# Token rows scattered as high and low fp16 halves, expert blocks loaded with a transposing transfer

## What is computed

```python
x = x + _layernorm(_L0_attn_ref(_layernorm(x, axis=-1), ...), axis=-1)
x = x + _layernorm(_L0_ffn_ref(_layernorm(x, axis=-1), ...), axis=-1)

# in _L0_ffn_ref: 8 experts, HIDDEN = 512, TOP_K = 2
shared = jnp.einsum('th,hd->td', jax.nn.silu(x_flat @ shared_w1.T), shared_w2.T)
top_k_gates, top_k_idx = jax.lax.top_k(x_flat @ gate_w.T, TOP_K)
top_k_gates = jax.nn.softmax(top_k_gates, axis=1)
h = jnp.einsum('td,ehd->teh', x_flat, experts_w1)
expert_out = jnp.einsum('teh,edh->ted', jax.nn.silu(h), experts_w2)
selected = jnp.einsum('ted,te->td', expert_out, gates)
return (shared + selected).reshape(B, S, D)
```

## Time and profile before

| | us |
|---|---|
| median of three runs | 606.42 |
| the profiled execution | 603.52 |
| its span, first to last instruction | 601.8 |
| TensorE busy | 465.4 |
| VectorE busy | 295.8 |
| GpSimd busy | 272.3 |
| ScalarE busy | 261.4 |

### The profile page before, as it was taken

The page is one execution under the profiler, slowest core; times in us unless marked ns, Lnnn a source line. Parts: engine busy times, 40 slices in busy tenths (PEclk is TensorE's granted clock), DMA queues, the critical chain, the costliest instruction groups (busy, mean ns, idle before and its releaser), DMA issues.

```text
span 601.8 us, 10616 instructions
## 1 busy us (share of the span) xinstructions
PE 465.4 (77%) x3392; PEld 360.3 (60%) x3392; DVE 295.8 (49%) x1258; ACT 261.4 (43%) x540; POOL 272.3 (45%) x408
## 2 busy tenths in 40 slices
PE   4799999999979998698625765597999899997000
PEld 3477766667655666476314544476999899887000
DVE  5887785786571477995444302300323222222273
ACT  3554544444544466554543312233444344443043
POOL 7200000110001366678878875500555655556593
PEclk9899999999999999988668877778999999999555
DMA  8920000000000000001010221345222222221621
GB/s 269 329 92 19 19 19 1 2 1 1 2 0 1 1 2 0 2 2 36 19 33 28 64 71 54 122 117 173 65 72 75 83 77 74 72 64 40 249 115 70
DMA packets 23221, 38.09 MB, mean 63 GB/s; under 512 B 4384, under 2 KB 14880, under 8 KB 22912
## 3 DMA queue, kind: packets, MB, share of 16 engines
q1 hardware_dynamic: 13248, 23.78, 12.2%
q0 software_dynamic: 4544, 9.45, 4.8%
q10 hardware_dynamic: 5376, 4.20, 2.1%
HBM read 21.74 MB, written 15.66 MB: 62 GB/s over the span
## 4 chain that ended last, share of the span: by engine, by line
PE 53%; POOL 17%; DVE 9%; another core or an unknown queue 7%; issue 6%; ACT 5%; DMA 2%; POOLq 0%; ACTq 0%; DVEq 0%; SPq 0%
POOL xs L505 5%; PE pPQ L895 4%; PE pPK L613 4%; PE pQKV L895 4%; PE pKV L688 3%; PE pPK L611 3%; PE pF L613 3%; PE pF L611 3%; PE pPK L612 3%; PE pF L612 2%; PE pQKV L811 2%; PE pPK L804 2%; POOL rs L449 2%; PE pQKV L857 2%
## 5 line engine op out<-in xcount | busy, mean ns | idle before, releaser
L578 POOL DMA_INDIRECT ys<-MID,PQT x78 | 75.7, 971 | 25.6 <-issue 25.6
L445 POOL TENSOR_TENSOR ve<-mv,eps 128x4 f32<-128x4 f32 x40 | 8.0, 201 | 164.8 <-DVE mv L1117 164.7
L505 POOL DMA_INDIRECT xs<-PL,SLOT x64 | 62.8, 981 | 19.8 <-issue 19.8
L611 PE MATMUL pPK<-XFH,E1H 128*128 128x512 f16 x32 | 15.5, 484 | 45.1 <-ACT HT L1041 25.5
L449 POOL TENSOR_TENSOR rs<-ve,halves 128x4 f32<-128x4 f32 x40 | 40.7, 1018 | 3.1
L438 POOL TENSOR_TENSOR held<-halves 128x1 f32<-128x1 f32 x47 | 9.1, 194 | 67.9 <-DVE MID L1424 58.6
L895 PE MATMUL pQKV<-E,HT 128*128 x320 | 39.1, 275 | 0.5 <-DVE MID L1424 0.5
L1424 DVE TENSOR_SCALAR MID<-pPQ,PQT 128x128 f32<-128x128 f32 x38 | 11.6, 346 | 55.7 <-remote 39.3
L895 PEld LDWEIGHTS pQKV<-E,HT 128*128 128x128 f32 x320 | 37.3, 192 | 1.0 <-issue 0.7
L895 PE MATMUL pPQ<-E,HT 128*128 x304 | 37.1, 275 | 0.4 <-DVE MID L1424 0.4
L895 PEld LDWEIGHTS pPQ<-E,HT 128*128 128x128 f32 x304 | 35.4, 192 | 0.9 <-issue 0.7
(11 more groups left out here) (258 smaller groups left out, 1309.2 us busy)
## 6 DMA issues: line engine op xcount, KB each, us to landing
PQT<-xs SPq DMA_DIRECT2D x39, 132.0 KB
PQT<-in_ew1T SPq DMA_DIRECT2D x1, 2304.0 KB, 10.7
E<-in_ew2T SPq DMA_DIRECT2D x1, 2304.0 KB, 10.6
X<-in_x SPq DMA_DIRECT2D x8, 256.0 KB, 6.0
HT<-in_ew1T SPq DMA_DIRECT2D x8, 256.0 KB, 5.9
sh<-PK ACTq DMA_DIRECT2D x8, 256.0 KB
PQT<-sh SPq DMA_DIRECT2D x8, 256.0 KB, 3.9
PQT<-ys SPq DMA_DIRECT2D x4, 512.0 KB
```

Source lines behind the costliest of these rows:

```text
L505: eng.indirect_dma_start(xs, bass.IndirectOffsetOnAxis(SLOT[:, g, t, a:a + 1], 0), PL[:, g, t, a, :], None).then_inc(s_scat[g], 16)
L578: eng.indirect_dma_start(ys, bass.IndirectOffsetOnAxis(XS[q][:, t, ID_AT:ID_AT + 1].bitcast(U32), 0), Y[q][:, t, :], None).then_inc(s_ysc[ ...
L611: nc.tensor.matmul(o, a[0], b_[0], start=True, stop=False)
```

## The change

- The token rows in `PL` now hold the fp16 high halves of 128 numbers, then the 128 low halves, in the same 512 bytes. At stage 14 VectorE writes the fp32 token into slot 1, and ScalarE writes its high half into slot 0. At stage 15 VectorE writes the low half there; at stage 16, once TensorE has transposed slot 1, VectorE copies high and low to slot 1. Scatters are the same in count and size.
- A block's load becomes two transfers: gates and row numbers only (16 bytes a row, 256 pieces), and a transposing transfer of the 256x256 halves into a ring `XB` of four blocks, which lies in `PK`. The transfer waits until the up-projection of four blocks ago is done.
- `turn_block`, `hi_block` and `lo_block` are gone; the up-projection waits for the transfers.
- SyncE's wait for the shared results' stores moves from behind the eighth load to ahead of the first.
- A partition now holds rows p and 128 + p of a block rather than 2p and 2p + 1.

```diff
+RING = 4
+    xs16 = xs.bitcast(F16)
-        XBH, XBL = (PK[:, i].rearrange("p c f -> p (c f)").bitcast(F16)[:, 0:2 * BW].rearrange("p (q s) -> p q s", q=2) for i in range(2))
+        XB = PK[:].rearrange("p i c f -> p (i c f)").bitcast(F16)[:, 0:RING * 2 * BW].rearrange(
+            "p (q i s) -> p q i s", q=RING, i=2)
+        PLH = PL[:].rearrange("p g t a w -> p (g t a w)").bitcast(F16).rearrange(
+            "p (g t a w) -> p g t a w", g=GB, t=T, a=TOPK)
...
@@ sync @@
             sp.wait_ge(s_tab, 13)
+            for h in range(2):
+                sp.wait_ge(s_shst[h], 16 * (NG // 2))
             for k in range(NBLK):
...
-                sp.dma_start(XS[q], xs[bass.ds(row, BW)].rearrange("(p a) w -> p a w", a=2)).then_inc(s_bx[q], 16)
+                sp.dma_start(XS[q][:, :, D:RW],
+                             xs[bass.ds(row, BW)].rearrange("(t p) w -> p t w", t=2)[:, :, D:RW]).then_inc(s_bx[q], 16)
+                wait(sp, s_u, 2 * (k - RING) + 2)
+                sp.dma_start_transpose(XB[:, k % RING], xs16[bass.ds(row, BW), 0:2 * D]).then_inc(s_bx[q], 16)
                 if k == UNROLL - 1:
-                    for h in range(2):
-                        sp.wait_ge(s_shst[h], 16 * (NG // 2))
...
@@ tensor @@
-                    turn(pKV, lambda t: PL[:, g, t, 0, 0:D]).then_inc(s_fT, 1)
+                    turn(pKV, lambda t: PL[:, g, t, 1, 0:D]).then_inc(s_fT, 1)
...
-            def turn_block(k):
-                q = k % UNROLL
-                wait(pe, s_bl, k - 1)
-                pe.wait_ge(s_bx[q], k // UNROLL * 16 + 16)
-                for t in range(2):
-                    m = nc.tensor.transpose(turned[k % 2][:, t * P:(t + 1) * P], XS[q][:, t, 0:D], ident[:])
-                m.then_inc(s_bT, 1)
...
-                    m = three(o, w, [XBH[:, k % 2, :], XBL[:, k % 2, :]])
+                    m = three(o, w, [XB[:, k % RING, i, :] for i in range(2)])
...
-                pe.wait_ge(s_bl, k + 1)
-                if k + 1 < NBLK:
-                    turn_block(k + 1)
+                pe.wait_ge(s_bx[k % UNROLL], k // UNROLL * 32 + 32)
                 up_block(k, ew)
@@ scalar @@
-                    A(PL[:, g, :, 1, 0:D], PL[:, g, :, 0, 0:D], ACT.Copy).then_inc(s_cpy, 1)
+                    A(PLH[:, g, :, 0, 0:D], PL[:, g, :, 1, 0:D], ACT.Copy).then_inc(s_rh, 1)
...
-            def hi_block(k):
-                wait(act, s_u, 2 * k - 2)
-                act.wait_ge(s_bT, k + 1)
-                A(XBH[:, k % 2, :], (pT, pKV)[k % 2][:, 0:BW], ACT.Copy).then_inc(s_bh, 1)
@@ vector @@
-                    norm(4, n, lambda t: PL[:, g, t, 0, 0:D], row(X, n))
+                    norm(4, n, lambda t: PL[:, g, t, 1, 0:D], row(X, n))
...
+                if k == 15:
+                    dve.wait_ge(s_rh, n + 1)
+                    v.tensor_tensor(PLH[:, g, :, 0, D:2 * D], PL[:, g, :, 1, 0:D], PLH[:, g, :, 0, 0:D],
+                                    ALU.subtract).then_inc(s_rl, 1)
                 if k == 16:
+                    dve.wait_ge(s_fT, n + 1)
+                    dve.wait_ge(s_rl, n + 1)
+                    v.tensor_copy(PLH[:, g, :, 1, 0:2 * D], PLH[:, g, :, 0, 0:2 * D]).then_inc(s_cpy, 1)
                     dve.wait_ge(s_xfh, n + 1)
...
-            def lo_block(k):
-                dve.wait_ge(s_bh, k + 1)
-                v.tensor_tensor(XBL[:, k % 2, :], (pT, pKV)[k % 2][:, 0:BW], XBH[:, k % 2, :],
-                                ALU.subtract).then_inc(s_bl, 1)
```

More of the change, by code:

```diff
@@ L271, in build @@
         s_pid, s_ids, s_cpy = sem("row_ids"), sem("ids_next"), sem("row_copied")
+        s_rh, s_rl = sem("row_hi"), sem("row_lo")
         s_rt, s_place, s_base, s_slot = (sem(n) for n in (
@@ L281, in build @@
         s_bx = [sem(f"rows_loaded{q}") for q in range(UNROLL)]
-        s_bT, s_bh, s_bl, s_u, s_si, s_do, s_y = (sem(n) for n in (
-            "block_turned", "block_hi", "block_lo", "block_up", "block_silu", "block_down", "block_result"))
+        s_u, s_si, s_do, s_y = (sem(n) for n in (
+            "block_up", "block_silu", "block_down", "block_result"))
         s_take = sem("result_taken")
@@ L584, in add_routed @@
             def add_routed(n):
-                pool.wait_ge(s_bx[n], 16 * len(range(n, NBLK, UNROLL)) + 16)
+                pool.wait_ge(s_bx[n], 32 * len(range(n, NBLK, UNROLL)) + 16)
                 y = routed[n]
@@ L868, in _ @@
             pe.wait_ge(s_sh, NG)
-            turned = [pT, pKV]
             outs = [pQKV, pPQ]
-            def turn_block(k):
-                q = k % UNROLL
-                wait(pe, s_bl, k - 1)
-                pe.wait_ge(s_bx[q], k // UNROLL * 16 + 16)
-                for t in range(2):
-                    m = nc.tensor.transpose(turned[k % 2][:, t * P:(t + 1) * P], XS[q][:, t, 0:D], ident[:])
-                m.then_inc(s_bT, 1)
             def up_block(k, ew):
@@ L897, in down_block @@
                 m.then_inc(s_do, 1)
-            turn_block(0)
             last = None
@@ L1058, in _ @@
             banks = [pF[0], pF[1], pPK[0], pPK[1]]
-            def hi_block(k):
-                wait(act, s_u, 2 * k - 2)
-                act.wait_ge(s_bT, k + 1)
-                A(XBH[:, k % 2, :], (pT, pKV)[k % 2][:, 0:BW], ACT.Copy).then_inc(s_bh, 1)
-            hi_block(0)
             for k in range(NBLK):
-                if k + 1 < NBLK:
-                    hi_block(k + 1)
                 for h in range(2):
@@ L1426, in result @@
                 s.then_inc(s_y, 1)
-            lo_block(0)
-            for k in range(NBLK):
-                if k + 1 < NBLK:
-                    lo_block(k + 1)
-                if k:
-                    result(k - 1)
+            for k in range(1, NBLK):
+                result(k - 1)
             result(NBLK - 1)
```

## The result

The kernel became slower: 618.08 us median (616.12 to 620.94, 4 runs) against 606.69 us (603.66 to 609.91, 4 runs) beside it on the same chip. The ratio is 1.019, 95% interval 1.012 to 1.026. The profiled execution took 616.28 us with a span of 614.5 us; before it was 603.5 with 601.8. The span's 12.7 us are what has to be explained.

What follows compares the result with a forecast made beforehand. TensorE was taken to bound the expert blocks, VectorE and GpSimd earlier stretches. By the profile 603.5 - 8.6 + 2.6 + 2.4 = 599.9 us, from the median 602.8; forecast 601.5, between the two, range 590 to 626.

Steps and rivals of the forecast that it cites:

- the slow transfer: Rival: in the blocks, the transposing transfer becomes the bound above 3.3 us a block; 627 at 4 us; chance 0.23.
- The 0.21 us a block between the two figures is about 8 us: In the blocks, 3.31 us undisturbed against 3.52 on average; TensorE's signals seen late during GpSimd's scatters, about 8 us.
- GpSimd's two-block cycle takes over: Rival: in the blocks, two blocks take 7.20 us whatever TensorE does; +3.0 us, 611 to 614 in all; chance 0.15.
- 78 transposes, -8.6 us: In the blocks, each of 39 loses two transposes on TensorE, 0.22 us a pair; -8.6 us.
- Start of the blocks, +2.6 us: First up-projection comes later, as SyncE's first row load waits for the last shared store; +2.6 us, bounds +2.5 and +5.
- Token stages, +2.4 us: In the VectorE-bound stretch, two copies and two subtractions delay GpSimd's chain; +2.4 us (2.2 to 3.4).
- Transfers hidden: In the blocks, row transfers take 1.8 us and SyncE's step 1.2 to 2 us, hidden below 3.3 us a block.
- Shared loads "up to 4 us once": Block 8's transfer queues behind the eight shared loads, lands by about 440 us, hidden; without cover, up to 4 us once.

Runs made afterwards that it cites:

- a_less: Changed kernel with the ring in its own place and two matmuls instead of three per up-projection product in the blocks; 607.17 us, ratio 0.998.
- a_half: Changed kernel with one of the two result scatters of each block left out; 608.58 us, ratio 0.997.
- b_half: Kernel before with one of the two result scatters of each block left out; 604.99 us, ratio 0.995.
- a_best: Changed kernel with ring apart, GpSimd's wait between a block's scatters, no GpSimd addition ahead of them, and the halves' copy on ScalarE; 590.89 us, ratio 0.978.
- b_gap: Kernel before with a GpSimd wait between a block's two scatters for the next block's down-projection; 596.19 us, ratio 0.984.
- b_gap_tok: Kernel before with GpSimd's wait between a block's two scatters and only the token part of the change; 598.22 us, ratio 0.987.
- a_nohold: Changed kernel with the ring in its own place and without GpSimd's small addition ahead of each block's scatters; 604.19 us, ratio 0.994.
- a_plain: Changed kernel with a plain load of the same bytes in place of each transposing one; 614.59 us, ratio 1.011.
- after_gap: Changed kernel as it is, with GpSimd's wait between a block's two scatters; 602.10 us, ratio 0.993.
- a_gap: Changed kernel with the ring in its own place and GpSimd's wait between a block's two scatters; 595.49 us, ratio 0.980.

## Why the prediction was wrong

The forecast was 601.5 us, 0.8% under the 606.42 of before; the kernel came out 1.9% slower. That 618.08 lies inside the range of 590 to 626 is luck: its upper part was there for the slow transfer, which did not come. By the profile 599.9 us were forecast and 616.28 measured. Of the 16.4 us between, 13.7 are the blocks, 3.3 the token stages and 0.3 the start, less 1.0 behind the blocks.

- **The blocks' stalls: the step that failed.** "The 0.21 us a block between the two figures is about 8 us" was carried over unchanged, so that 3.30 us a block was forecast; 3.66 was measured, 13 us in 36 blocks. I had seen late signals every 7.20 us and put them down as a fixed cost beside the 3.31. They are a property of GpSimd's cycle and grow to fill most of what TensorE saves: a pair of blocks takes 7.20 us late in the kernel before, 7.32 on average in the changed one and 7.13 in a_less, where TensorE by itself needs 6.63, 6.20 and 5.32. Before, the average of 3.52 was held down by the first 24 blocks, which lost 4.0 us to stalls, against 3.4 in the last twelve. The rival "GpSimd's two-block cycle takes over" is what happened. Its price of +3.0 us was low (measured +5.1, with runs of three blocks, the clock and the shared loads in it), and its sign, strict 7.2 us pairs from the first blocks, came only in part: from the second block on (434.83 us) GpSimd issues runs of four, 7.3 us apart, but runs of two and of six mix in later. I gave it 0.15, because the earlier trace rows showed no pairs up to 439 us. What I should have read is GpSimd's own rows in the quiet part. They show that it was already falling behind: four blocks in 14.69 us, 3.67 each, while TensorE made one in 3.31. Not all of that is GpSimd's own work: in each pair it waits 1.6 to 1.8 us for a late result. Timeline of GpSimd in the kernel before, the first instruction of a block and of the fourth one after it:

```profile
445.99 0.21 POOL L438 TENSOR_TENSOR held<-halves 128x1 f32<-128x1 f32 x1
...
460.68 0.21 POOL L438 TENSOR_TENSOR held<-halves 128x1 f32<-128x1 f32 x1
```

- **78 transposes, -8.6 us: right as work, worth nothing as time.** The spacing fell from 3.315 to 3.10 us. Only with the cause of the stalls gone (a_half against b_half, a_best against b_gap) did it show in the blocks.
- **Start of the blocks, +2.6 us: right**, 2.9 measured. SyncE's part was 1.4 us, the transposing transfer 2.98 us from issue to use (420.90 to 423.88) where I took 0.3 and 2.6.
- **Token stages, +2.4 us: right for the edit, too small for the trace.** VectorE's subtraction takes 0.69 us (0.68 forecast) and its copy 0.42 (0.5). GpSimd's chain starts at 268.51 instead of 264.30, and the last store 5.7 us late. b_gap_tok showed 3.1 us and 2 us in the end. The eleven traces with the same code in these stages have the last shared store anywhere from 413.1 to 421.2 us (up to 418.6 but for a_less and a_nohold); three of the old code have it at 410.9 to 411.2. What makes the new stages scatter by 5 us and more was not tested and stays open. It is about half of the 5.7.

```profile
L1311 DVE TENSOR_TENSOR PL<-PL x8: 679/692/1645, 231.2 to 351.2; 128x512 f16<-128x512 f32 x8
...
L1316 DVE COPY PL<-PL x8: 364/419/565, 241.6 to 352.1; 128x1024 f16<-128x1024 f16 x8
```

- **Transfers hidden: right in steady blocks.** SyncE's step is 2.5 us, not 1.2 to 2: the transposing issue takes three times a plain one (1.22 us against 0.37 in a_plain), and table read and register steps come on top. Queue 1 carries 39456 - 13248 = 26,208 packets more, 672 a block, near the 640 of the forecast (512 half rows and 256 pieces instead of 128). But they do not cost the 38 ns of the earlier trace rows: 14.0% of 16 x 614.5 us against 12.2% of 16 x 601.8 is 202 us of engine time, 7.7 ns a packet and 0.3 us a block on 16 engines, not 1.8. The rival of a transposing transfer as the bound, to which I gave 0.23, did not come: the wait for them in steady blocks is nil. The Trainium skill ("DMA: Bandwidth & Descriptors", Latency and other measured facts) has 261 GB/s for a transposing transfer with a non-contiguous middle dimension, an estimated 0.5 us for 128 KB. The trace neither confirms nor contradicts this, since the 2.98 us hold fixed parts that no row separates.
- **Shared loads "up to 4 us once":** 2.6 us in the changed kernel, 6.6 in after_gap and 6.8 in a_half, nothing when they were spread out. The forecast saw the place; it called the loads hidden because it let block 8's transfer land by 440 us, while SyncE only issued it at 445.85.

## What to carry to other kernels

If a stall returns with a fixed period, find the engine whose cycle has that period before counting its time as a constant: here GpSimd's some 7.2 us for two blocks was the bound, and most of the work taken off TensorE turned into waiting. Measure the period's floor by halving the suspected work in both versions; that one pair of runs told more than the whole trace. And where an engine issues indirect scatters in long runs, try a wait that spaces them against TensorE's own rhythm: it cost two lines and brought 1.6%, about as much as the 78 transposes were meant to.

## What the runs showed of the hardware that I had not expected

- How late VectorE sees a signal of TensorE depends on how many indirect scatters GpSimd has just issued and with what pauses. With none yet issued in the blocks it is under 0.1 us (before: down-projection over at 421.24, VectorE at 421.28). In a run that begins after a pause of 2.1 us it is 0.1 us during the second scatter and 1.4 us during the fourth (a_nohold). In a steady row of two scatters and pauses of 0.8 to 0.9 us it is 1.1 to 1.2 us, seen 0.6 us behind the run (a_gap, 440 us); with blocks 3.31 us apart and a pause of 1.0 us, 0.1 us (b_gap, 502 us). Behind six it was 3.6 us, seen 1.3 us behind the run (the changed kernel); ScalarE and SyncE waited as long or longer there. One reading is that something piles up during a run and drains in the pauses. No run shows what it is (the scatters' 128 pieces, their bytes, or GpSimd's writing of them).
- After 6 us in which TensorE was busy for 3.48, the granted clock was 0.66 over the next 5 us; one late signal so cost 3.1 us of stall and 1.7 us of slower work.
- A transposing transfer of 256 rows of 512 bytes takes SyncE 1.22 us to issue (the changed kernel), a plain one of the same bytes 0.37 (a_plain).
